# Transposing DMAs queued by ScalarE instead of SyncE, with a third column turned by DMA

## The chip, the cores and the metric

The kernel runs on one core of one Trainium2 chip. The metric is the device time of one execution in microseconds (us); the median of three executions of the kernel before is 1655.98 us (1655.0 to 1656.74).

## The reference

One layer of cross attention and one layer of an expert-choice feed-forward network, both with a residual, in float32:

```python
x = x + xattn(layernorm(x), ctx)            # x: 2 x 2048 x 512, ctx: 2 x 77 x 384, 8 heads of 64
x = x + ffn(layernorm(x))

def ffn(x, gate_w, w1, w2):                 # 8 experts, 512 -> 2048 -> 512
    probs = softmax(einsum('ntd,ed->nte', x, gate_w), -1)
    g, m = top_k(probs.transpose(0, 2, 1), k)          # k = 2 * 2048 / 8 = 512 tokens of each batch
    xin = x[batch_idx, m]
    h = gelu(einsum('nekd,edf->nekf', xin, w1))
    h = einsum('nekf,efd->nekd', h, w2)
    return zeros.at[batch_idx, m].add(g[..., None] * h)
```

A column is one (batch, expert) pair: 512 tokens, their gates, and the expert's weights. There are 16.

## The kernel before

After the attention stage the layer-normed rows lie in HBM as `xn2_rows`. The expert stage has two parts. Four columns are **plain** (`PLAIN`, experts 0 and 1 of both batches), done one after another, i = 0 to 3, each in 16 slots (n = 16 i + f, f = 0 to 15). The other six experts are done as **pairs** x = 0 to 5, both batches at once, in groups of a quarter of the hidden size (n = 0 to 23, four for each pair). All products use a high and a low part of both operands, three matmuls for one.

In a slot TensorE makes `up(n)` (12 matmuls into bank 4 or 5) and then `down(n - 2)` (12 matmuls); at f = 15 the last two down products follow at once, and at f = 0 and 1 there is none. `up(n)` waits for the gelu of slot n - 2, which frees its bank. ScalarE's order in a slot is: the high parts of the weights of slot n + 2 (`act_weights`, two copies), the gelu of slot n (line 1743), and then what else is put into that slot. VectorE makes the low parts and the low part of the gelu (line 1935), which the down product waits for.

A column's rows are gathered from HBM by GpSimd (`pool_gather`, `gather_pair`) with the token on the partition, and the products want them transposed. Column 0 and column 2 (the third) are transposed on TensorE: `pe_token_chunk` (line 1732), four transposes for each of four chunks, for the third column at the end of slots 27 to 30 (`TURNS_1`, `turn`), and ScalarE and VectorE copy each chunk out of PSUM as its high and low part (`act_token_chunk`, `dve_token_chunk`).

The keys in `TURNED` are transposed by DMA instead: columns 1 and 3, pair 0 (`(0, 1)` and `(0, 0)`, one key for each batch), and the later pairs. A DMA transposes two-byte words, so this goes in steps, each in two halves a = 0, 1 (two of the four row tiles each):

- `act_split` (line 1490): ScalarE separates the 16-bit halves of the float words into `planes`, two instructions, and raises `r_split`.
- `sp_turn` (line 1497): SyncE waits for `r_split` and issues the transposing DMA of 512 KB within SBUF, which raises `r_turn[a]` when it has landed.
- `act_words` (line 1507): ScalarE waits for `r_turn[a]` and joins the halves back into float words, four instructions; `r_word` tells that the rows are ready.
- For a plain column, `act_turned_chunk` and `dve_turned_chunk` then make the high and low parts of its four chunks.

For column i + 1 the splits stand in slots f = 10 and 11 of column i, the words in 12 and 13, the chunks in 14 and 15. For pair 0 the splits are in slots 49, 50 (batch 1) and 52, 53 (batch 0), the words in 51, 52 and 54, 55. Of a later pair, one batch each is turned in the second and third group of the pair before: after the first three weight copies of the next group comes the first split, then four more copies, the second split, and both words.

SyncE's queue is in order (`sp_experts`): weight loads (`sp_weights`, two of 1 MB for every four slots) and the transposing DMAs stand in one list. For pair 0 the transposes of a batch stand ahead of the weight loads of the fourth column's third and fourth quarter; in the late stage the loads of group n + 2 wait for the words of the key whose buffers they overwrite.

GpSimd's queue is in order as well: gathers, the scatter-adds of finished columns (line 1597), and ten lists of tokens and gates for the later pairs, each written by 16 indirect DMAs (`write_lists`, line 1612): one list, the second column's gather, two lists, scatter, one list, the third column's gather, two lists, scatter, the fourth's gather, the gather of (0, 1), three lists, the gather of (0, 0), scatter, one list.

Of the kernel before, what the change touches and what calls it, by code (L numbers as in the profile page):

```python
# [14 lines left out]
P = 128  # L15
B, S, D = 2, 2048, 512
# [25 lines left out]
def xattn_expert_choice(nc, x, ctx, wq, wk, wv, wo, bo, gate_w, w1, w2, out):  # L42
# [8 lines left out]
    with top:  # L51
# [1410 lines left out]

        r_split, r_word = sem("r_split"), sem("r_word")
        r_turn = [sem(f"r_turn{a}") for a in range(2)]
        TURNED = ((1,), (3,), (0, 1), (0, 0)) + tuple((x, b) for x in range(1, NS) for b in range(B))

        def turned(key):

# [22 lines left out]
                                            rows[:, h, 2 * a:2 * a + 2], ACT.Copy)  # L1491
            last.then_inc(r_split, 1)

        def sp_turn(sp, key, a):
            halves, out = planes_of(key)
            sp.wait_ge(r_split, turned(key) - 1 + a)
            sp.dma_start(out[:, a * 4 * CAP:(a + 1) * 4 * CAP].rearrange("p (j t) -> p j t", t=P),
                         halves[:, 2 * a:2 * a + 2].rearrange("p q c -> p (q c)"), transpose=True).then_inc(r_turn[a], 16)

        def act_words(act, key, a):  # L1500
            words = rows_of(key).bitcast(U16).rearrange("p c (q t h) -> p h q c t", h=2, t=P)
# [6 lines left out]
            last.then_inc(r_word, 1)  # L1508


        SPLIT_AT, WORDS_AT, CHUNKS_AT = (10, 11), (12, 13), {14: (0, 1), 15: (2, 3)}

        PAIR_SPLIT_AT = {(0, 1): (49, 50), (0, 0): (52, 53)}
        PAIR_WORDS_AT = {(0, 1): (51, 52), (0, 0): (54, 55)}
# [24 lines left out]

        assert rounds_in(ROUNDS_AT[-1])[1] == ROUNDS - 1  # L1540
        VALS_AT = CHOICE_AT + 4
        TURNS_1 = tuple(range(KF // 2 + 3, KF - 1))
# [4 lines left out]
        hot_of = {q: m for m, q in HOT_AT.items()}  # L1547
        found_of = {q: m for m, q in FOUND_AT.items()}

        def turn(n):  # L1550

            i, f = divmod(n, KF)
            return TURNS_1.index(f) if i == 1 and f in TURNS_1 else None

        def sp_experts(sp):
            for gg in range(2, G * len(PLAIN)):
                if gg >= 4 * G - 2:
                    for a in range(2):
                        sp_turn(sp, (0, 4 * G - 1 - gg), a)
                sp_weights(sp, gg)  # L1560
                if gg in (G, 3 * G):
                    for a in range(2):
                        sp_turn(sp, (gg // G,) if gg == G else (3,), a)
            for n in range(NG):
                e, g = NPE + n // G, n % G
                key = ((n - 2) // G + 1, (n - 2) % G - 1) if n >= 2 else None
                if key in TURNED:
                    sp.wait_ge(s_Wl, NPR * (n - 2) + 3)
                    sp.wait_ge(s_sum, 4 * (n - 1))
                    for a in range(2):  # L1570
                        sp_turn(sp, key, a)
                    sp.wait_ge(r_word, turned(key))
                if n < 2:
                    sp.wait_ge(f_w2l, NPL - GF * (1 - n))
                else:
                    sp.wait_ge(s_Wl, NPR * (n - 2) + 3)
                    sp.wait_ge(s_sum, 4 * (n - 1))
                sp.dma_start(w1_raw[:, n % 2], group_w1(e, g)).then_inc(s_raw1[n % 2], 16)
                if n >= 2:
                    sp.wait_ge(s_v2l, GF * (n - 1))  # L1580
                if key in TURNED:
                    for a in range(2):
                        sp.wait_ge(r_turn[a], 8 * turned(key))
                sp.dma_start(w2_raw[:, n % 2], group_w2(e, g)).then_inc(s_raw2[n % 2], 16)
            sp.wait_ge(s_scat, 16 * ND * NS)

        def pool_experts(pool):
# [72 lines left out]
            pool_gather(pool, 1)  # L1660
            write_lists(1, 3)
            scatter(0)
            write_lists(3, 4)
            pool_gather(pool, 2)
            write_lists(4, 6)
            scatter(1)
            pool_gather(pool, 3)
            gather_pair(0, 1)
            write_lists(6, 9)
            gather_pair(0, 0)  # L1670
            scatter(2)
            write_lists(9, 10)
            for x in range(E - NPE - LX):
                read_lists(x)
            scatter(len(PLAIN) - 1)
# [29 lines left out]
                                    ALU.subtract).then_inc(f_w2l, 1)  # L1705

        def act_token_chunk(act, i, k, bank):
            act.wait_ge(f_tr, i // 2 * KD + k + 1)
# [27 lines left out]
        def act_experts(act):  # L1736
            def slot(n):
# [10 lines left out]
                if n == 2:  # L1748
                    act_gate_exp(act, NBLK - 1)
                    act_normalise(act, X1[:, u], rs2, nb2, XN2[:, u], g_nb2, a_xn2, NBLK - 1)  # L1750
                k = turn(n - 1)
                if k is not None:
                    act_token_chunk(act, (n - 1) // KF + 1, k, 6)
                i, f = divmod(n, KF)
                if (i + 1,) in TURNED:
                    if f == SPLIT_AT[0]:
                        act.wait_ge(f_rows, 16 * CT * (i + 2))
                    if f in SPLIT_AT:
                        act_split((i + 1,), SPLIT_AT.index(f))
                    if f in WORDS_AT:  # L1760
                        act_words(act, (i + 1,), WORDS_AT.index(f))
                    for k in CHUNKS_AT.get(f, ()):
# [105 lines left out]
            def group(n):  # L1868
# [21 lines left out]
                if n + 1 < NG:  # L1890
                    for idx in W_ORDER[0:3]:
                        w_high(n + 1, idx)
                    if key in TURNED:
                        act.wait_ge(s_rows[key[1]], 16 * CT * (x + 2))
                        act.wait_ge(s_v2l, GF * (n + 1))
                        act_split(key, 0)
                    for idx in W_ORDER[3:]:
                        w_high(n + 1, idx)
                    if key in TURNED:
                        act_split(key, 1)  # L1900
                        act_words(act, key, 0)
                        act_words(act, key, 1)
                if last:
# [20 lines left out]
        def dve_experts(dve):  # L1924
            def slot(n):
# [5 lines left out]
                if n >= S3:  # L1931
# [5 lines left out]
                k = turn(n - 1)  # L1937
                if k is not None:
                    dve_token_chunk(dve, (n - 1) // KF + 1, k, 6)
                i, f = divmod(n, KF)  # L1940
                if (i + 1,) in TURNED:
                    for k in CHUNKS_AT.get(f, ()):
# [225 lines left out]
        def pe_experts(pe):  # L2168
# [33 lines left out]
            def slot(n):  # L2202
# [154 lines left out]
```

## Time and profile before

| | |
|---|---|
| median of three executions | 1655.98 us |
| the profiled execution, its own time | 1658.91 us |
| its span, first to last instruction | 1657.1 us |
| TensorE busy | 1641.7 us (99%) |
| VectorE busy | 1074.7 us (65%) |
| ScalarE busy | 942.8 us (57%) |
| GpSimd busy | 476.6 us (29%) |
| mean granted TensorE clock | 0.997 |

Busy times are of one execution. Issuing a DMA, waiting and branching are not counted as busy, though an engine that issues is held by it. Overlapping matmuls are counted once. The expert stage starts at about 305 us, the groups of pairs at about 660.

### The profile page before, as it was taken

To read this page: it belongs to the slowest core of one execution; us is meant where nothing else is said; L and a number is where in the kernel's file an instruction comes from. 1 tells how busy PE (TensorE), PEld (TensorE's weight loads), DVE (VectorE), ACT (ScalarE), POOL (GpSimd) and SP (SyncE) were. 2 spreads that over 40 slices of the span, in tenths; PEclk is the share of its full clock that TensorE was granted. 3 is DMA by queue.
4 is the path that set the end of the run, shared out by engine and by line. 5 is a ranking of instruction groups with operands and counts; after the bars stand their busy time and mean duration, and the time that the engine had idled before them with its cause. 6 is when DMAs were issued, how large, how long until landed. Compare 5 with 4: busy or idle time off the path is not lost.

```text
span 1657.1 us, 22979 instructions
## 1 busy us (share of the span) xinstructions
PE 1641.7 (99%) x8348; PEld 1405.0 (85%) x8348; DVE 1074.7 (65%) x1938; ACT 942.8 (57%) x2045; POOL 476.6 (29%) x537
## 2 busy tenths in 40 slices
PE   9999999999999999999999999999999999999997
PEld 9999999878888878888888888888888888888886
DVE  7555697777764438655765586558655856686663
ACT  5678776735333565466546664666466646654441
POOL 3233233377477770300230033003200420040003
PEclk9999999999999999999999999999999999999999
DMA  3243436365426694412442244234323432351004
GB/s 134 77 140 115 153 119 226 127 152 127 131 54 180 128 178 151 102 29 85 136 108 53 84 119 102 76 85 101 95 77 96 96 89 77 102 97 57 26 1 51
DMA packets 140357, 171.27 MB, mean 103 GB/s; under 512 B 68141, under 2 KB 69321, under 8 KB 140249
## 3 DMA queue, kind: packets, MB, share of 16 engines
q1 hardware_dynamic: 120441, 136.04, 27.5%
q0 software_dynamic: 19776, 33.78, 11.3%
q8 instruction: 65, 1.06, 0.3%
q14 instruction: 43, 0.35, 0.1%
q10 hardware_dynamic: 32, 0.03, 0.0%
HBM read 121.42 MB, written 33.72 MB: 94 GB/s over the span
## 4 chain that ended last, share of the span: by engine, by line
PE 95%; ACT 1%; DMA 1%; DVE 1%; issue 0%; POOL 0%; POOLq 0%; SPq 0%; ACTq 0%; DVEq 0%
PE ps L2282 10%; PE ps L2280 10%; PE ps L2281 10%; PE ps L2260 9%; PE ps L2258 9%; PE ps L2259 9%; PE ps L1254 4%; PE ps L1255 4%; PE ps L1256 4%; PE ps L2195 3%; PE ps L2182 3%; PE ps L2184 3%; PE ps L2183 3%; PE ps L2196 3%; PE ps L2197 3%; DMA turned_planes<-planes 1%
## 5 line engine op out<-in xcount | busy, mean ns | idle before, releaser
L2280 PE MATMUL ps<-v2h,hhS 128*128 128x512 f32 x768 | 298.9, 389 | 0.0
L2282 PE MATMUL ps<-v2h,hlS 128*128 128x512 f32 x768 | 298.9, 389 | 0.0
L2281 PE MATMUL ps<-v2l,hhS 128*128 128x512 f32 x768 | 298.9, 389 | 0.0
L1646 POOL DMA_INDIRECT out_dram<-YS,tok_pair x40 | 86.4, 2161 | 682.8 <-DVE YS L2091 673.7
L2259 PE MATMUL ps<-Tl,Wh 128*128 128x512 f32 x672 | 261.5, 389 | 0.0
L2258 PE MATMUL ps<-Th,Wh 128*128 128x512 f32 x672 | 261.5, 389 | 0.0
L2260 PE MATMUL ps<-Th,Wl 128*128 128x512 f32 x672 | 261.5, 389 | 0.0
L1612 POOL DMA_INDIRECT list<-pairs,list_at x160 | 171.1, 1069 | 49.3 <-issue 48.2
L1833 ACT ACTIVATE v2h<-w_raw 128x512 fp32r<-128x512 f32 x96 | 57.5, 622 | 215.0 <-PE ps L2282 215.0
L2281 PEld LDWEIGHTS ps<-v2l,hhS 128*128 128x128 f32 x768 | 144.2, 188 | 30.0
L2282 PEld LDWEIGHTS ps<-v2h,hlS 128*128 128x128 f32 x768 | 144.2, 188 | 29.8
L2280 PEld LDWEIGHTS ps<-v2h,hhS 128*128 128x128 f32 x768 | 144.2, 188 | 29.8
L1851 ACT ACTIVATE hhS<-hfS 128x512 fp32r<-128x512 f32 x144 | 91.0, 632 | 127.8 <-DVE hfS L2060 66.4
L2071 DVE TENSOR_TENSOR hlS<-hfS,hhS 128x512 fp32r<-128x512 f32 x192 | 128.0, 687 | 46.8 <-ACT hfS L1852 46.8
L2091 DVE SCALAR_TENSOR_TENSOR YS<-ps,tok_pair,YS 128x512 f32<-128x512 f32 x120 | 88.8, 749 | 102.2 <-PE ps L2282 102.2
L2259 PEld LDWEIGHTS ps<-Tl,Wh 128*128 128x128 f32 x672 | 126.2, 188 | 26.2
L2260 PEld LDWEIGHTS ps<-Th,Wl 128*128 128x128 f32 x672 | 126.2, 188 | 26.1
L2258 PEld LDWEIGHTS ps<-Th,Wh 128*128 128x128 f32 x672 | 126.2, 188 | 26.1
L2182 PE MATMUL ps<-eTh,w1h 128*128 128x512 f32 x248 | 98.1, 395 | 2.2 <-ACT hf L1743 2.2
L2195 PE MATMUL ps<-w2h,hh 128*128 128x512 f32 x248 | 98.1, 396 | 0.0
L1743 ACT ACTIVATE hf<-ps 128x512 f32<-128x512 f32 x64 | 38.2, 597 | 103.6 <-PE ps L2184 103.6
L2183 PE MATMUL ps<-eTl,w1h 128*128 128x512 f32 x248 | 97.1, 392 | 0.0
(297 smaller groups left out, 3692.9 us busy)
## 6 DMA issues: line engine op xcount, KB each, us to landing
w_raw<-in_L_ffn_w_dram SPq DMA_DIRECT2D x80, 1024.0 KB, 7.3
XB<-in_x_dram SPq DMA_DIRECT2D x16, 512.0 KB, 4.0
XR<-in_x_dram SPq DMA_DIRECT2D x16, 512.0 KB, 6.4
out_dram<-X SPq DMA_DIRECT2D x16, 512.0 KB, 5.0
xn_rows<-XN SPq DMA_DIRECT2D x16, 512.0 KB, 5.3
list<-pairs,list_at POOLq DMA_INDIRECT x160
w_raw<-in_L_xattn_Wq_dram SPq DMA_DIRECT2D x1, 1024.0 KB, 8.4
wo_sb<-in_L_xattn_Wo_dram SPq DMA_DIRECT2D x2, 512.0 KB, 11.0
```

The costliest lines, as they stand in the source:

```text
L1612: pool.indirect_dma_start(out=lists[b * E + NPE + LX + x], out_offset=bass.IndirectOffsetOnAxis(ap=list_at[:, b, x, t:t + 1], axis=0), in_ ...
L1851: nc.scalar.activation(hhS[:, b, f], src, ACT.Gelu)
L2071: nc.vector.tensor_tensor(hlS[:, b, f], hfS[:, b, f], hhS[:, b, f].bitcast(F32), ALU.subtract).then_inc(s_hid, 1)
L2182: nc.tensor.matmul(ps[:, 4 + n % 2, :], wh, th, start=(k == 0), stop=False)
L2183: nc.tensor.matmul(ps[:, 4 + n % 2, :], wh, tl, start=False, stop=False)
L2195: nc.tensor.matmul(ps[:, c, :], th, wh, start=(f == 0), stop=False)
L2258: nc.tensor.matmul(ps[:, bank, :], wh, th, start=(idx in OPENS and k == 0), stop=False, **go_on)
L2259: nc.tensor.matmul(ps[:, bank, :], wh, tl, start=False, stop=False, **go_on)
L2260: last = nc.tensor.matmul(ps[:, bank, :], wl, th, start=False, stop=(k == 1), **go_on)
L2280: nc.tensor.matmul(ps[:, bank, :], th, wh, start=(t == 0), stop=False)
L2281: nc.tensor.matmul(ps[:, bank, :], th, wl, start=False, stop=False)
L2282: last = nc.tensor.matmul(ps[:, bank, :], tl, wh, start=False, stop=(t == GF - 1))
```

## The change

ScalarE takes over the transposing DMAs: `sp_turn` becomes `act_turn`, and every call of `act_split` has it right behind. SyncE's list keeps the weight loads alone. The third column (key `(2,)`) joins `TURNED`: its chunks no longer pass TensorE, its splits both stand in slot 29 (f = 13 of column 1), its words in 30 and 31, its four chunks in 31. GpSimd writes two lists in place of one ahead of the third column's gather, and the last list moves from behind the third scatter to ahead of the gather of (0, 0). In the late stage ScalarE takes over SyncE's two waits for the weight buffers, for work of the group before.

```diff
-        TURNED = ((1,), (3,), (0, 1), (0, 0)) + tuple((x, b) for x in range(1, NS) for b in range(B))
+        TURNED = ((1,), (2,), (3,), (0, 1), (0, 0)) + tuple((x, b) for x in range(1, NS) for b in range(B))
...
-        def sp_turn(sp, key, a):
+        def act_turn(act, key, a):
             halves, out = planes_of(key)
-            sp.wait_ge(r_split, turned(key) - 1 + a)
-            sp.dma_start(out[:, a * 4 * CAP:(a + 1) * 4 * CAP].rearrange("p (j t) -> p j t", t=P),
+            act.wait_ge(r_split, turned(key) - 1 + a)
+            act.dma_start(out[:, a * 4 * CAP:(a + 1) * 4 * CAP].rearrange("p (j t) -> p j t", t=P),
...
-        SPLIT_AT, WORDS_AT, CHUNKS_AT = (10, 11), (12, 13), {14: (0, 1), 15: (2, 3)}
+        SPLIT_AT = {i: {13: (0, 1)} if i == 1 else {10: (0,), 11: (1,)} for i in range(3)}
+        WORDS_AT = {i: {14: (0,), 15: (1,)} if i == 1 else {12: (0,), 13: (1,)} for i in range(3)}
+        CHUNKS_AT = {i: {15: (0, 1, 2, 3)} if i == 1 else {14: (0, 1), 15: (2, 3)} for i in range(3)}
...
             for gg in range(2, G * len(PLAIN)):
-                if gg >= 4 * G - 2:
-                    for a in range(2):
-                        sp_turn(sp, (0, 4 * G - 1 - gg), a)
                 sp_weights(sp, gg)
-                if gg in (G, 3 * G):
-                    for a in range(2):
-                        sp_turn(sp, (gg // G,) if gg == G else (3,), a)
...
                 if key in TURNED:
-                    sp.wait_ge(s_Wl, NPR * (n - 2) + 3)
-                    sp.wait_ge(s_sum, 4 * (n - 1))
-                    for a in range(2):
-                        sp_turn(sp, key, a)
                     sp.wait_ge(r_word, turned(key))
...
             scatter(0)
-            write_lists(3, 4)
+            write_lists(3, 5)
             pool_gather(pool, 2)
-            write_lists(4, 6)
+            write_lists(5, 7)
             scatter(1)
             pool_gather(pool, 3)
             gather_pair(0, 1)
-            write_lists(6, 9)
+            write_lists(7, 10)
             gather_pair(0, 0)
             scatter(2)
-            write_lists(9, 10)
...
-                k = turn(n - 1)
-                if k is not None:
-                    act_token_chunk(act, (n - 1) // KF + 1, k, 6)
                 i, f = divmod(n, KF)
                 if (i + 1,) in TURNED:
-                    if f == SPLIT_AT[0]:
+                    for a in SPLIT_AT[i].get(f, ()):
                         act.wait_ge(f_rows, 16 * CT * (i + 2))
-                    if f in SPLIT_AT:
-                        act_split((i + 1,), SPLIT_AT.index(f))
...
+                        act_split((i + 1,), a)
+                        act_turn(act, (i + 1,), a)
...
                     if n in PAIR_SPLIT_AT[key]:
                         act_split(key, PAIR_SPLIT_AT[key].index(n))
+                        act_turn(act, key, PAIR_SPLIT_AT[key].index(n))
...
                         act.wait_ge(s_v2l, GF * (n + 1))
+                        act.wait_ge(s_Wl, NPR * n + 3)
+                        act.wait_ge(s_sum, 4 * (n + 1))
                         act_split(key, 0)
+                        act_turn(act, key, 0)
                     for idx in W_ORDER[3:]:
                         w_high(n + 1, idx)
                     if key in TURNED:
                         act_split(key, 1)
+                        act_turn(act, key, 1)
...
-                if turn(n) is not None:
-                    pe_token_chunk(pe, n // KF + 1, turn(n), 6)
```

## Rows read from the trace of the kernel before

**Rows 1.** The page, busy time, share and instructions of TensorE and the others.

```profile
PE 1641.7 (99%) x8348; PEld 1405.0 (85%) x8348; DVE 1074.7 (65%) x1938; ACT 942.8 (57%) x2045; POOL 476.6 (29%) x537
```

**Rows 2.** Timeline of TensorE, 603 to 615: start, us, instruction, [idle before].

```profile
603.58 0.39 PE L2182 MATMUL ps<-eTh,w1h 128*128 128x512 f32 x1
...
608.79 0.39 PE L2197 MATMUL ps<-w2h,hl 128*128 128x512 f32 x1
611.36 0.77 PE L2182 MATMUL ps<-eTh,w1h 128*128 128x512 f32 x1 [2.18 <-ACT hf L1743]
...
614.81 0.40 PE L2184 MATMUL ps<-eTh,w1l 128*128 128x512 f32 x1
```

**Rows 3.** Windows: length, PE, PEld, DVE, ACT, POOL busy, clock, DMA share, GB/s.

```profile
610.00:615.00 5.00, 3.64 (x9) 2.96 (x10) 2.32 (x4) 3.11 (x5) 0.30 (x1) 0.66 1.26 136
```

**Rows 4.** The chain of waits, 580 to 616: start, us, what.

```profile
584.51 0.52 ACT w1h L1692
...
585.55 0.49 ACT hf L1743
...
589.76 15.34 DMA turned_planes<-planes
```

**Rows 5.** Timeline of ScalarE, slots 49 to 53, for (0, 1).

```profile
582.51 2.00 ACT L1490 ACTIVATE planes<-XR 128x1024 uint16<-128x1024 uint16 x2
...
598.69 2.67 ACT L1507 ACTIVATE XR<-turned_planes 128x512 uint16<-128x512 uint16 x4 [7.91 <-DMA turned_planes<-planes]
...
610.63 0.59 ACT L1743 ACTIVATE hf<-ps 128x512 f32<-128x512 f32 x1
```

**Rows 6.** Timeline of TensorE at one of the third column's four chunks.

```profile
471.49 0.65 PE L1732 MATMUL ps<-ident,XB 128*128 128x128 f32 x4
...
472.22 0.39 PE L2183 MATMUL ps<-eTl,w1h 128*128 128x512 f32 x1
```

**Rows 7.** Transposing DMAs: issue ns min/median/max; fourth column's issue and words; SyncE's wait.

```profile
L1497 SPq DMA_TRANSPOSE w_raw<-w_raw x20: 1752/1904/2028, 732.5 to 1430.0; - x20
L1497 SPq DMA_TRANSPOSE turned_planes<-planes x8: 1987/3090/8527, 363.9 to 613.1; - x8
...
543.73 5.00 SPq L1497 DMA_TRANSPOSE turned_planes<-planes  x1
...
553.04 2.66 ACT L1507 ACTIVATE XB<-turned_planes 128x512 uint16<-128x512 uint16 x4 [0.35 <-DMA turned_planes<-planes]
...
SPq L1496 <- ACT w_raw L1490: 416.3, 10, 54.7
```

**Rows 8.** Timelines, slot 29: ScalarE's gelu, VectorE's low part; TensorE, next expert's start.

```profile
468.97 0.60 ACT L1743 ACTIVATE hf<-ps 128x512 f32<-128x512 f32 x1 [2.57 <-PE ps L2184]
...
470.14 0.69 DVE L1935 TENSOR_TENSOR hl<-hf,hh 128x512 fp32r<-128x512 f32 x1
...
489.34 0.39 PE L2182 MATMUL ps<-eTh,w1h 128*128 128x512 f32 x1
```

**Rows 9.** Timeline of ScalarE in a late group, second split to the next group.

```profile
734.37 2.00 ACT L1490 ACTIVATE w_raw<-XB 128x1024 uint16<-128x1024 uint16 x2
738.48 5.17 ACT L1507 ACTIVATE XB<-w_raw 128x512 uint16<-128x512 uint16 x8 [2.11 <-DMA w_raw<-w_raw]
749.26 1.15 ACT L1833 ACTIVATE v2h<-w_raw 128x512 fp32r<-128x512 f32 x2 [5.62 <-PE ps L2282]
```

**Rows 10.** GpSimd: third column's gather, third column's scatter, and all list writes grouped.

```profile
441.75 1.19 POOL L943 DMA_INDIRECT XB<-xn_rows,tok_idx  x1 [16.68 <-DVE tok_gate L823]
...
582.20 1.63 POOL L1597 DMA_INDIRECT out_dram<-Y,tok_idx  x1 [0.30 <-issue]
...
L1612 POOL DMA_INDIRECT list<-pairs,list_at x160 | 171.1, 1069 | 49.3 <-issue 48.2
```

**Rows 11.** Timeline at the start: first plain DMA issue on SyncE and on ScalarE.

```profile
0.81 0.42 SPq L236 DMA_DIRECT2D ctx_sb<-in_ctx_dram  x1
0.81 0.61 ACTq L417 DMA_DIRECT2D gw_sb<-in_L_ffn_gate_w_dram  x1
```

More of the change, by code:

```diff
@@ L1492, in act_split @@
             last.then_inc(r_split, 1)
-        def sp_turn(sp, key, a):
+        def act_turn(act, key, a):
             halves, out = planes_of(key)
-            sp.wait_ge(r_split, turned(key) - 1 + a)
-            sp.dma_start(out[:, a * 4 * CAP:(a + 1) * 4 * CAP].rearrange("p (j t) -> p j t", t=P),
-                         halves[:, 2 * a:2 * a + 2].rearrange("p q c -> p (q c)"), transpose=True).then_inc(r_turn[a], 16)
+            act.wait_ge(r_split, turned(key) - 1 + a)
+            act.dma_start(out[:, a * 4 * CAP:(a + 1) * 4 * CAP].rearrange("p (j t) -> p j t", t=P),
+                          halves[:, 2 * a:2 * a + 2].rearrange("p q c -> p (q c)"), transpose=True).then_inc(r_turn[a], 16)
         def act_words(act, key, a):
@@ L1541, in xattn_expert_choice @@
         VALS_AT = CHOICE_AT + 4
-        TURNS_1 = tuple(range(KF // 2 + 3, KF - 1))
         HOTS = [q for q in range(VALS_AT + 1, 3 * KF + 4)
@@ L1548, in xattn_expert_choice @@
         found_of = {q: m for m, q in FOUND_AT.items()}
-        def turn(n):
-            i, f = divmod(n, KF)
-            return TURNS_1.index(f) if i == 1 and f in TURNS_1 else None
         def sp_experts(sp):
             for gg in range(2, G * len(PLAIN)):
-                if gg >= 4 * G - 2:
-                    for a in range(2):
-                        sp_turn(sp, (0, 4 * G - 1 - gg), a)
                 sp_weights(sp, gg)
-                if gg in (G, 3 * G):
-                    for a in range(2):
-                        sp_turn(sp, (gg // G,) if gg == G else (3,), a)
             for n in range(NG):
@@ L1707, in act_token_chunk @@
         def act_token_chunk(act, i, k, bank):
-            act.wait_ge(f_tr, i // 2 * KD + k + 1)
+            act.wait_ge(f_tr, i * KD + k + 1)
             nc.scalar.activation(eTh[i % 2][:, k, :], ps[:, bank, :], ACT.Copy).then_inc(f_eTh, 1)
@@ L1750, in slot @@
                     act_normalise(act, X1[:, u], rs2, nb2, XN2[:, u], g_nb2, a_xn2, NBLK - 1)
-                k = turn(n - 1)
-                if k is not None:
-                    act_token_chunk(act, (n - 1) // KF + 1, k, 6)
                 i, f = divmod(n, KF)
                 if (i + 1,) in TURNED:
-                    if f == SPLIT_AT[0]:
+                    for a in SPLIT_AT[i].get(f, ()):
                         act.wait_ge(f_rows, 16 * CT * (i + 2))
-                    if f in SPLIT_AT:
-                        act_split((i + 1,), SPLIT_AT.index(f))
-                    if f in WORDS_AT:
-                        act_words(act, (i + 1,), WORDS_AT.index(f))
-                    for k in CHUNKS_AT.get(f, ()):
+                        act_split((i + 1,), a)
+                        act_turn(act, (i + 1,), a)
+                    for a in WORDS_AT[i].get(f, ()):
+                        act_words(act, (i + 1,), a)
+                    for k in CHUNKS_AT[i].get(f, ()):
                         act_turned_chunk(act, i + 1, k)
@@ L1936, in slot @@
                                         ALU.subtract).then_inc(f_h, 1)
-                k = turn(n - 1)
-                if k is not None:
-                    dve_token_chunk(dve, (n - 1) // KF + 1, k, 6)
                 i, f = divmod(n, KF)
                 if (i + 1,) in TURNED:
-                    for k in CHUNKS_AT.get(f, ()):
+                    for k in CHUNKS_AT[i].get(f, ()):
                         dve_turned_chunk(dve, i + 1, k)
```

## Prediction

> **What bounds the kernel now.** I read the page first: TensorE is busy for 1641.7 of 1657.1 us [rows 1], so the change can pay only by taking work off TensorE or by removing a place where TensorE waits. The waits of TensorE, next, name one such place that the change touches: the fourth expert, in the slots 51 to 55. TensorE's rows there [rows 2] show the last down product starting at 608.79 and the next up product at 611.36, where 609.02 was due (the slot from 603.58 to 608.79 has 24 matmuls, so they start 0.227 apart). That is 2.34 us idle. Then eight matmuls take until 614.81, 3.45 us where 1.82 was due, 1.63 more: the granted clock of this stretch is 0.66, between the levels of 1.2 and 2.4 GHz, and what came before it is the idle time [rows 2, 3]. Together 3.97 us. The chain of waits gives the cause [rows 4]: the second transposing DMA of pair (0, 1) took 15.34 us from issue to landing, ScalarE stood waiting for both, 7.91 us for the first alone, and so the gelu of slot 53, which frees the PSUM bank for that up product, came only at 610.63 [rows 5].
>
> The reader is to see in [rows 5] that a gelu is not needed at once. It started 0.73 us before the up product that it let go. So the gelu of slot 53 may start until 609.02 - 0.73 = 608.3 at no cost, and each slot before it until 5.44 us (24 x 0.227) earlier. All costs below are weighed against such limits.
>
> **Part 1, the third column leaves TensorE.** Four times four transposes go. One group starts at 471.49 and the second matmul after it at 472.22 [rows 6]: 0.73, where two matmuls without it are 0.23 apart, so 0.50. The three others of this kind in the trace are a little shorter; I take 0.45 each, 1.8 us in all, and this is on the path, since nothing hides TensorE's own work. **-1.8 us.**
>
> **Part 2, ScalarE queues the DMAs.** There are 28 now and 30 after. An issue held SyncE 1.75 to 2.03 us in the late stage (20 of them) and 1.99 to 8.53 us, median 3.09, in the early stage (8 of them) [rows 7]. ScalarE is now held instead. No issue on ScalarE of this kind is in the trace; of plain ones the first took 0.61 there and 0.42 on SyncE [rows 11]. So an issue in the late stage costs between 1.9 and 1.9 x 0.61 / 0.42 = 2.8 us; I take 1.9, as the same descriptors are made. The move alone lands nothing earlier: SyncE stood waiting for ScalarE's split before the first DMA of each of the ten late pairs [rows 7], not the other way round.
>
> What is held behind it on ScalarE, in the late stage: four weight copies, then the second half's split, then the words. Now the second split starts at 734.37, is done after 1.9 at 736.3, the words start at 738.48 after a wait of 2.11 for the landing, end at 743.65, and ScalarE's next work is let go by TensorE only at 749.26 [rows 9]. With two issues of 1.9 the words start at 736.3 + 3.8 = 740.1, past the landing of the first half. The first half was issued when its split was done, four copies of 0.52 before 734.37, at 732.3, so it took 6.2 to land; at that pace the second, issued at 738.2, lands at 744.4 and its words end at 746.9. Of 5.6 us of cover, 3.3 are used. With 2.8 each it still fits; from about 3.7 each on TensorE would stall in each of the ten groups. **0 us**, at both ends.
>
> By the Trainium skill (DMA: Bandwidth & Descriptors, Issuing engines are not separate DMA queues) DMAs of ScalarE and SyncE run on the same DMA engines and interleave, and issuing from both saves only issue time on a sequencer. By that rule the change has no transfer to gain here, only issue time to move onto a busier engine; SyncE's wait in [rows 7] agrees; by the rule alone the sum would be part 1, 1654.2.
>
> **Part 3, the third column on ScalarE.** Both splits and both issues now stand in slot 29, words in 30 and 31, four chunk copies in 31. With TensorE 0.9 earlier by then, slot 29's gelu is at 468.97 - 0.9 = 468.1 [rows 8]. From there gelu 0.49, split 2.0, issue j0, split 2.0, issue j1, weights 1.04, gelu, words 2.5, weights, gelu of slot 31 at 477.7 + j0 + j1 (durations from [rows 4, 5]). The next expert was at 489.34 [rows 8], now 487.5; the last down product before it starts 2.7 earlier, at 484.8, and wants the gelu 1.9 before (gelu at 468.97, VectorE's low half done at 470.83 [rows 8]), at 482.9. So j0 + j1 may be 5.2. Clean: 3.8, no cost. As in the fourth column, whose first issue took 5.00 [rows 7] and whose second, queued on an idle ring, I put at 2.5: 7.5, a stall of 2.3 and perhaps 1.6 of slow clock behind it, 3.9. SyncE's weight load of that slot is in flight then, but on its own queue; in the fourth column it stood ahead of that 5.00. I take 2.6 + 2.0 = 4.6: **0 us**, ends 0 and +3.9.
>
> **Part 4, lists.** One list more is written ahead of the third gather. GpSimd stood 16.68 us before that gather, waiting for its indices [rows 10]; a list takes 22 (171.1 and 49.3 over ten lists), so the gather and all behind it come 5 us later. Its rows are first read in slot 29, some 20 us after: nothing. But pair (0, 0)'s gather and the scatter of the third column, first issue at 582.20 [rows 10], also come 5 us later, to about 587, while the pair's splits come 1.8 earlier. The list that ran beside the pair's second transpose is gone. SyncE no longer holds the weight load behind the transposes, so it starts at about 580, beside the first one.
>
> **Part 5, the pair in slots 49 to 54.** In the old clock: split at 582.51, first issue i0 at 584.5, weights, gelu, second split, second issue i1 at 588.0 + i0, weights and gelu (1.53 per slot, [rows 4]), words of 2.5 at 593.6 + i0 + i1, then pair (0, 0)'s split and issue i2, weights, and the gelu of slot 53 at 599.2 + i0 + i1 + i2. Limit 608.3, so the three may take 9.1. Also the second transpose must land by 608.3 - 1.0 - i2 - 2.0 - 2.5 = 602.8 - i2. Bounds: all clean, 5.7, no stall. As on SyncE now, 5.2, 8.5 and 3.0, sum 16.7: 7.6 late, 9.0 by slot 54, where a fourth issue of 3.1 is added. I take the first, now ahead of the scatter, at 3.0, the second, inside it, at 5.2, the third at 1.9: 10.1, 1.0 over. Its landing, issued at 591.0, takes 9.3 (the fourth column's first half, 543.73 to 553.04 [rows 7]) to 15.3 [rows 4]: 600.3 to 606.3 against a limit of 600.9, so 0 to 5.4 late. Middle 3.0, plus 1.6 of slow clock: 4.6 against 4.0 now, **+0.6 us**. In short, the wait for the landing shrinks and the issues take its place: this is what is late next.
>
> **Sum.** -1.8 + 0 + 0 + 0.6 = -1.2 us. The profiled execution took 1658.91, 2.9 over the median 1655.98, perhaps with a longer stall; on it 1657.7, on the median **1654.8 us**.
>
> **Rivals.** *The pair's stall goes* (A): clean issues and landing under the limit; -1.8 - 4.0 = -5.8, 1650.2. For it: the list beside it and the queue ahead are gone. Against: the scatter stays. *ScalarE is held by the issues themselves* (B), slower: i0 + i1 + i2 as on SyncE, 16.7; from a sum of 13.3 on (9.1, the 4.0 of now less 1.6, and the 1.8) the kernel is slower; loss 9.0 + 1.6 against 4.0, net +4.8, 1660.8 (1662.4 with a second slow stretch). For it: 8.53 us on SyncE beside that very scatter [rows 7], and the weight load now runs beside the first one. Against: the first is out of the scatter, and ScalarE's ring holds no loads. *The third column stalls* (C): forecast + 3.9 = 1658.7. *An issue costs ScalarE over 3.7 us in the late stage* (D): at 5.0, 2.5 x 10 more, 1680; against it [rows 11].
>
> By the Trainium skill (DMA: Bandwidth & Descriptors, Queues, rings and completion order) each DMA engine takes turns between the queues that have work for it, packet by packet. By that rule the pair's transposes, now on a queue of their own, would share with the weight load instead of standing before it, which favours B's price for the first issue; no run here shows a load and a transpose on two queues.
>
> **Chances.** Forecast 0.47, A 0.24, B 0.15, C 0.11, D 0.03. Under 0.2% (3.3 us, about what a measurement of this kernel can tell from no change) lie the forecast and most of C. Faster 0.26 (A and a little of the forecast), slower 0.22 (B, D, some of C with a long pair), same 0.52. The range of 8 in 10 goes from A, 1650.2, to B, 1661; D and B's far end are left out.
>
> **What would show it.** Right: no transposes into PSUM in slots 27 to 30; transposing issues on ScalarE's queue near 1.9 us from 730 us on; in the ten late groups a wait of ScalarE for TensorE before the copy of v2h still over 2 us; TensorE idle between 600 and 620 by 1 to 5 us with the clock below 1 behind it. Wrong: no idle time there (A); early issues of 5 us and more on ScalarE with gelu of slot 51 already late (B); idle TensorE at 480 to 490 (C); TensorE waits in the late groups (D).

## The result, and the profile after

The changed kernel takes 1674.03 us (median of four executions, 1672.69 to 1674.66); the kernel before, run beside it, 1656.36 us (1655.0 to 1658.2). The ratio is 1.0105, interval 1.0087 to 1.0122: slower by about 1%, where 1654.8 was forecast with a range up to 1661.0. The profiled execution took 1674.66 us, its span is 1672.7 us against 1657.1, so 15.6 us are to be explained. (The medians differ by 17.7 us; the traced execution of the kernel before was 2.6 us above its median.)

First the page and two groups of TensorE's waits between 300 and 700 us (us in total, times, longest):

```profile
PE 1640.1 (98%) x8332; PEld 1401.3 (84%) x8332; DVE 1074.8 (64%) x1938; ACT 950.8 (57%) x2057; POOL 480.5 (29%) x537
...
PE ps L2167 <- ACT hf L1729: 13.0, 2, 9.8
PE ps L2180 <- DVE hl L1923: 3.4, 2, 2.5
```

TensorE is busy 1.6 us less than before [rows 1], and in these two groups it waits 16.4 us where [rows 2] showed one wait of 2.18. The timeline of TensorE shows the places:

```profile
476.43 0.39 PE L2167 MATMUL ps<-eTh,w1h 128*128 128x512 f32 x1
...
484.56 0.50 PE L2180 MATMUL ps<-w2h,hh 128*128 128x512 f32 x1 [2.53 <-DVE hl L1923]
...
488.45 0.50 PE L2180 MATMUL ps<-w2h,hh 128*128 128x512 f32 x1 [0.87 <-DVE hl L1923]
...
604.59 0.77 PE L2167 MATMUL ps<-eTh,w1h 128*128 128x512 f32 x1 [9.77 <-ACT hf L1729]
...
609.72 0.40 PE L2180 MATMUL ps<-w2h,hh 128*128 128x512 f32 x1
...
632.23 0.47 PE L2167 MATMUL ps<-eTh,w1h 128*128 128x512 f32 x1 [3.27 <-ACT hf L1729]
```

After the wait of 9.77 us, twelve matmuls take 609.72 - 604.59 = 5.13 us where 12 x 0.227 = 2.73 was due: 2.4 more. The windows (length; PE, PEld, DVE, ACT and POOL busy; granted clock; DMA share; GB/s) give a clock of 0.55 there, between the two levels of 1.2 and 2.4 GHz, and what came before it is the idle time, as in [rows 3]:

```profile
605.00:610.00 5.00, 5.00 (x14) 3.85 (x14) 1.41 (x4) 2.61 (x5) 0.00 (x0) 0.55 1.04 164
630.00:640.00 10.00, 7.78 (x27) 6.29 (x28) 5.48 (x10) 9.55 (x18) 0.00 (x0) 0.83 0.27 59
```

In the same way the 13 matmuls from 632.23 take 1.7 us more than due. ScalarE's timeline says what TensorE waited for (start, us, instruction, idle before):

```profile
470.46 5.95 ACTq L1497 DMA_TRANSPOSE turned_planes<-planes  x1
...
478.49 2.77 ACTq L1497 DMA_TRANSPOSE turned_planes<-planes  x1
...
586.50 16.21 ACTq L1497 DMA_TRANSPOSE turned_planes<-planes  x1
602.82 0.63 ACT L1678 ACTIVATE w1h<-w_raw 128x512 fp32r<-128x512 f32 x1 [16.34 <-issue]
...
603.87 0.58 ACT L1729 ACTIVATE hf<-ps 128x512 f32<-128x512 f32 x1
...
606.37 2.31 ACTq L1497 DMA_TRANSPOSE turned_planes<-planes  x1
...
610.26 2.67 ACT L1507 ACTIVATE XR<-turned_planes 128x512 uint16<-128x512 uint16 x4
...
618.84 1.59 ACTq L1497 DMA_TRANSPOSE turned_planes<-planes  x1
...
624.03 6.32 ACTq L1497 DMA_TRANSPOSE turned_planes<-planes  x1
```

The first issue of pair (0, 1) held ScalarE 16.21 us. Slot 50's gelu stood behind it, came at 603.87, and TensorE went on 0.72 us later. The words at 610.26 show no wait: at the pair nothing is late by landing any more, everything by issuing. The three long issues (5.95, 16.21, 6.32) are those beside which another queue had just begun. SyncE's timeline, then GpSimd's:

```profile
466.61 0.37 SPq L851 DMA_DIRECT2D w_raw<-in_L_ffn_w_dram  x1
...
584.28 0.37 SPq L851 DMA_DIRECT2D w_raw<-in_L_ffn_w_dram  x1
...
622.46 0.37 SPq L851 DMA_DIRECT2D w_raw<-in_L_ffn_w_dram  x1
...
585.47 1.15 POOL L1622 DMA_INDIRECT XB<-xn_rows,tok_idx  x1 [0.30 <-issue]
...
590.69 1.63 POOL L1584 DMA_INDIRECT out_dram<-Y,tok_idx  x1 [0.30 <-issue]
```

A load of 2 MB starts 1.6 to 3.9 us ahead of each of the three, and around the one of 16.21 us GpSimd's gather and scatter start as well. In the late groups all is quiet: twenty issues, no wait of TensorE, and ScalarE's wait for TensorE before its copy of v2h still 195.8 us in all, where it had been 215.0 in the kernel before.

```profile
L1497 ACTq DMA_TRANSPOSE w_raw<-w_raw x20: 1580/1865/2889, 747.9 to 1447.3; - x20
...
ACT v2h L1817 <- PE ps L2265: 195.8, 23, 16.7
```

The sum of the stretches: -1.9 (the third column; the up product of slot 31 starts at 476.43 where it started at 478.33, and in slot 22, at 425.35, the two timelines had been 0.06 apart), -4.0 (the wait and slow clock of before), +4.0 (third column: 3.4 idle, the rest its slower start), +9.77 + 2.4 (slot 50's gelu), +3.27 + 1.7 (slot 53's): 15.2 of the 15.6 us.

That the timelines are level in slot 22 hides one loss more. The traced execution of the changed kernel enters the expert stage 1.7 us earlier than that of the kernel before, and it gives this back behind the second column's first issue, which held ScalarE 3.57 us: VectorE, next, idled 3.29 us for ScalarE's late weight copy, and so TensorE waited for VectorE at a small matmul of the token choice.

```profile
362.19 3.57 ACTq L1497 DMA_TRANSPOSE turned_planes<-planes  x1
...
375.10 0.19 PE L694 MATMUL ps<-cnt,ones_bf 128*128 128x24 bf16 x1 [1.41 <-DVE cnt L688]
```

### The profile page after: what moved, and what is told of

Its sections match the earlier page's. It is cut to its first block, busy times and chain, and to the rows that moved or that the text cites. A ratio compares the mean times of both kernels' runs of the same rounds, so it can differ in the third digit from the quotient of the medians.

```text
span 1672.7 us, 22962 instructions
## 1 busy us (share of the span) xinstructions
PE 1640.1 (98%) x8332; PEld 1401.3 (84%) x8332; DVE 1074.8 (64%) x1938; ACT 950.8 (57%) x2057; POOL 480.5 (29%) x537
## 4 chain that ended last, share of the span: by engine, by line
PE 92%; ACT 3%; ACTq 2%; DVE 1%; issue 0%; DMA 0%; POOL 0%; POOLq 0%; SPq 0%
PE ps L2263 10%; PE ps L2264 10%; PE ps L2265 10%; PE ps L2242 9%; PE ps L2241 9%; PE ps L2243 9%; PE ps L1254 4%; PE ps L1255 4%; PE ps L1256 4%; PE ps L2167 3%; PE ps L2169 3%; PE ps L2168 3%; PE ps L2180 3%; PE ps L2182 3%; PE ps L2181 3%; ACTq L1497 2%
## 5 line engine op out<-in xcount | busy, mean ns | idle before, releaser
L1599 POOL DMA_INDIRECT list<-pairs,list_at x160 | 175.1, 1095 | 49.3 <-issue 48.2
L1817 ACT ACTIVATE v2h<-w_raw 128x512 fp32r<-128x512 f32 x96 | 57.4, 622 | 195.8 <-PE ps L2265 195.8
L2169 PE MATMUL ps<-eTh,w1l 128*128 128x512 f32 x248 | 98.0, 395 | 0.0
```

What stands on the lines that cost most here:

```text
L1599: pool.indirect_dma_start(out=lists[b * E + NPE + LX + x], out_offset=bass.IndirectOffsetOnAxis(ap=list_at[:, b, x, t:t + 1], axis=0), in_ ...
L2169: last = nc.tensor.matmul(ps[:, 4 + n % 2, :], wl, th, start=False, stop=(k == KD - 1))
```

## The experiments

The theory after this reading: what costs is that the issuing instruction lasts longer while the DMA engines are busy with other queues, and that moving it gave up an order. On SyncE's list the pair's transposes stood ahead of a weight load, which therefore began behind them; on ScalarE's they begin beside it, and ScalarE's gelu waits behind the issue. Rivals: the new list order on GpSimd; the issue on ScalarE as such; the late groups.

Beside these versions the kernel before took 1658.65 to 1659.38 us, some 3 us more than beside the changed kernel, while the expected times were set against its 1656; so each time is to be read by its ratio.

**The engine alone.** The kernel before, with `sp_turn` made `act_turn`, with the two late waits that go with it, and nothing else (third column on TensorE, lists as before).

```diff
-        def sp_turn(sp, key, a):
+        def act_turn(act, key, a):
...
                     if n in PAIR_SPLIT_AT[key]:
                         act_split(key, PAIR_SPLIT_AT[key].index(n))
+                        act_turn(act, key, PAIR_SPLIT_AT[key].index(n))
...
```

> The kernel before with one part of the change alone: ScalarE queues the transposing DMAs right behind the splits, SyncE keeps the weight loads. Third column on TensorE and lists in the old order. Theory (queueing by ScalarE beside load, gather and scatter is the loss): the pair's issues take 8 to 16 us in all more than clean ones, 1660 to 1668 us. Rival (lists in the new order bring gather and scatter onto the transposes): 1655 to 1658 us.

1670.54 us, ratio 1.0068 (1.0051 to 1.0085): the upper end of what was expected (1668 to 1656 is 1.007). The first issue of (0, 1) took 10.83 us and that of (0, 0)'s second half 5.93, each with a load begun just before (583.64 and 617.42), and TensorE waited 4.38 and 3.87 us behind them:

```profile
585.86 10.83 ACTq L1497 DMA_TRANSPOSE turned_planes<-planes  x1
...
618.99 5.93 ACTq L1497 DMA_TRANSPOSE turned_planes<-planes  x1
```

So the move of the queue alone makes the kernel slower, without lists or third column.

**The engine undone.** The changed kernel with every transpose back on SyncE; the third column's, like the pair's, ahead of the weight load of its slot.

```diff
             for gg in range(2, G * len(PLAIN)):
+                ahead = {2 * G + 1: (2,), 4 * G - 2: (0, 1), 4 * G - 1: (0, 0)}.get(gg)
+                if ahead:
+                    for a in range(2):
+                        sp_turn(sp, ahead, a)
                 sp_weights(sp, gg)
...
```

> The changed kernel with one part undone: SyncE queues all transposing DMAs again, those of the third column and of pair 0 ahead of the weight load of that slot. The third column stays off TensorE and the lists stay in the new order. Theory (ScalarE held by issues is the loss): the transposes on TensorE are saved, 1.8 us, the stall of the pair is at most the 4 us of before, so 1650 to 1655 us. Rival (the new order of lists and scatter, or the third column itself, is the loss): 1665 us or more.

1654.43 us, ratio 0.9971 (0.996 to 0.9983): faster than the kernel before, by 0.3%, and by the ratios 1.3% below the changed one. Its span is 1651.6, and TensorE's only wait in the plain columns is one of 0.2 us that the kernel before has too. SyncE's two issues of (0, 1) take 5.18 us in all with the pause between them: the load begins behind them, at 587.86, and the gather only with the second, at 586.25. Those of (0, 0) take 9.22, beside the lists that GpSimd reads; that is no shorter than in the changed kernel (1.59 and 6.32), but nobody stands behind them except the load:

```profile
582.63 5.18 SPq L1497 DMA_TRANSPOSE turned_planes<-planes  x2
601.06 9.22 SPq L1497 DMA_TRANSPOSE turned_planes<-planes  x2
```

**The late half kept, the plain columns undone.** As the last one, but the twenty late issues stay on ScalarE.

```diff
                         act_split(key, 0)
+                        act_turn(act, key, 0)
                     for idx in W_ORDER[3:]:
                         w_high(n + 1, idx)
                     if key in TURNED:
                         act_split(key, 1)
+                        act_turn(act, key, 1)
```

> The plain experts' transposes queued by SyncE, those of the third column and the pair ahead of the weight load of their slot; the late groups' twenty queued by ScalarE as in the changed kernel; the new list order and the third column by DMA kept. Theory (the late half of the change is free, because nothing else moves while those issues run, 1.6 to 2.0 us each, and ScalarE had idle time there): the same as with SyncE everywhere, 1652 to 1656, ratio to the kernel before 0.996 to 0.999, with the late issues at 1.6 to 2.1 us and no TensorE wait in the late groups. Rival (the late issues take ScalarE's time from the scaling work and cost some of the 20 x 1.8 us): 1657 to 1670.

1654.39 us, ratio 0.9974 (0.9964 to 0.9984), the same as with SyncE throughout. Twenty of the thirty issues may stand on either engine. The whole loss is in the ten of the plain columns.

**A transfer put beside the late issues.** The changed kernel, with two copies of 1 MB in HBM that nobody reads, begun by SyncE as each late pair's first half is split.

```diff
...
                 if key in TURNED:
+                    sp.wait_ge(r_split, turned(key) - 1)
+                    for h in range(2):
+                        sp.dma_start(spare[h], w2_flat[h]).then_inc(s_spare[h], 16)
                     sp.wait_ge(r_word, turned(key))
```

> The changed kernel with a cost added to measure it by itself: in the ten late groups with transposes SyncE also queues two copies of 1 MB within HBM when the first split is done, so that their packets run beside the transposing DMAs that ScalarE queues; nothing else of the late stage uses the DMA engines then but the weight loads behind the words. Theory (turns between queues, packet by packet): the late issues of 1.6 to 2.0 us grow to 3 to 7 where the copy runs beside them, and the landing comes later by as much. Rival (only GpSimd's gather and scatter hold an issue): they stay at 1.6 to 2.0 us.

The first issue of each late pair now takes 5.58 to 5.80 us, one 10.50; the median over all twenty (first halves and second) goes from 1865 to 5042 ns:

```profile
L1497 ACTq DMA_TRANSPOSE w_raw<-w_raw x20: 1770/5042/10497, 746.6 to 1456.2; - x20
```

So the length of an issue is made by what else is under way, in a place where it had been about 1.9 us. TensorE waited 1.91 us behind the issue of 10.50, for which VectorE had stood 7.26 us without ScalarE's weight copy; 0.46 and 0.83 us came some 30 us behind two other pairs of issues, and their cause was not followed. So the cover of a late group holds one issue of 5.6 us. The time, 1679.87 us, is one execution; its ratio to the kernel before is 1.0123 where the changed kernel has 1.0105, some 3 us more, and the three waits add up to 3.2.

**Loads held until the landing.** The changed kernel, with SyncE's load of the three slots waiting for both transposed halves; then, in addition, GpSimd's scatter waiting for those of (0, 1); then, apart from these, GpSimd's gather and scatter held and the loads free.

```diff
+                behind = {2 * G + 1: (2,), 4 * G - 2: (0, 1), 4 * G - 1: (0, 0)}.get(gg)
+                if behind:
+                    for a in range(2):
+                        sp.wait_ge(r_turn[a], 8 * turned(behind))
                 sp_weights(sp, gg)
```

> The changed kernel, ScalarE queues, but SyncE issues three of its weight loads (those of slots 29, 49 and 53) only after both halves of the transposes of that stretch have landed. Theory (the DMA engines take turns between the queues packet by packet, so each 256-byte packet of a transpose waits behind a 2-KB packet of the load, and ScalarE is held until about 700 of the 2048 are through): the third column's first issue falls from 5.95 to 1.6 to 2.5 us, pair (0, 0)'s second from 6.32 to under 2.5, pair (0, 1)'s first from 16.2 to 5 to 9, since gather and scatter remain; 1653 to 1661 us. Rival (GpSimd's gather and scatter alone hold it): pair (0, 1)'s first issue stays over 12 us, and 1664 us or more.

1666.6 us, ratio 1.0049 (1.0029 to 1.0069), by the ratios 0.56% less than the changed kernel; 1661 or less was expected. The issues became short: (2,)'s first 1.94 instead of 5.95, (0, 1)'s first 1.94 instead of 16.21. The second is below the 5 to 9 expected, as GpSimd's gather began only behind it, at 587.86. But (0, 1)'s second half, begun into the gather and scatter, took 6.62 to issue, and its words waited for the landing:

```profile
584.93 1.94 ACTq L1497 DMA_TRANSPOSE turned_planes<-planes  x1
...
590.53 6.62 ACTq L1497 DMA_TRANSPOSE turned_planes<-planes  x1
...
607.50 2.65 ACT L1507 ACTIVATE XR<-turned_planes 128x512 uint16<-128x512 uint16 x4 [4.62 <-DMA turned_planes<-planes]
```

TensorE waited 7.99 us at 618.13. Next, the scatter held too:

```diff
             gather_pair(0, 0)
+            for a in range(2):
+                pool.wait_ge(r_turn[a], 8 * turned((0, 1)))
             scatter(2)
```

> As the kernel with the loads held, and GpSimd issues the third column's scatter, too, only after both halves of pair (0, 1) have landed; the gather of (0, 0) stays beside them. Theory: all early issues under 4 us, idle TensorE in slots 51 to 55 under 2 us, 1649 to 1654 us. If the first issue of the pair still takes over 8 us, neither loads nor scatter are its cause.

1660.52 us, ratio 1.0018 (1.0002 to 1.0034), a further 6 us less, but 1654 was missed: the load and the scatter that had been held began together at 602.4 and 603.1, and (0, 0)'s first issue, 606.96, fell between them with 7.69 us; TensorE waited 9.47 us at 616.47 (in the traced execution, whose 1665.01 us are 4.5 above the median, so how much of this wait the median one has is not shown). The other way round:

```diff
             write_lists(7, 10)
+            for a in range(2):
+                pool.wait_ge(r_turn[a], 8 * turned((0, 1)))
             gather_pair(0, 0)
```

> The changed kernel, but GpSimd's gather of (0,0), and what is behind it, wait until both transposed halves of (0,1) have landed; SyncE's load of that slot is not held, so the first issue of (0,1) has one other queue beside it where it had two. Theory (the issue is held until about a third of its packets have gone, and the packets take turns with each queue that has some): the first issue of (0,1), 16.2 us with two queues beside it, 5.0 to 8.5 us, as the two that had the load alone beside them (5.95 and 6.32); TensorE's wait of 9.8 us behind it under 2.5 us; the time 1659 to 1667, as what remains is the third column's and (0,0)'s long issues. Rival (the weight load alone holds it): over 12 us, and the time over 1670.

(0, 1)'s first issue took 7.44 us, as expected with one other queue beside it where there were two, and TensorE waited 0.99 us behind it. The time was not as expected: 1673.18 us, ratio 1.009 (1.0072 to 1.0108). The held gather came late for (0, 0)'s split (a wait of 2.46 us), and (0, 0)'s issues took 4.52 and 6.78:

```profile
589.08 7.44 ACTq L1497 DMA_TRANSPOSE turned_planes<-planes  x1
...
614.72 4.52 ACTq L1497 DMA_TRANSPOSE turned_planes<-planes  x1
...
622.84 6.78 ACTq L1497 DMA_TRANSPOSE turned_planes<-planes  x1
...
621.07 0.77 PE L2169 MATMUL ps<-eTh,w1h 128*128 128x512 f32 x1 [6.05 <-ACT hf L1731]
```

In these three, each issue of the third column and the pair is short where nothing is begun beside it and long where something is; holding a transfer moved the meeting to the next transpose.

**The order given back to ScalarE.** SyncE's three loads wait until ScalarE has begun the slot behind the second issue: behind the issues, not behind the landing, as on SyncE's own list.

```diff
+                behind = {2 * G + 1: 29, 4 * G - 2: 50, 4 * G - 1: 53}.get(gg)
+                if behind:
+                    sp.wait_ge(f_w1h, behind + 4)
                 sp_weights(sp, gg)
```

> The changed kernel, ScalarE queueing every transpose, but SyncE's weight load of the third column's slot and of the pair's two slots waits until ScalarE has begun the slot after the second half's issue, so that the load stands behind both issues, as it does on SyncE's own queue in the kernel before, but not behind their landing. Theory (what was lost is the order that one queue gave, not the engine): (2,)'s two issues 1.9 to 2.5 us each, the first of (0,1) 1.9 to 3, its second 2 to 5 (beside the scatter), those of (0,0) 2 to 6; TensorE's waits from 430 to 700 us 0 to 3 in all where the changed kernel has 16; the time 1652 to 1658. Rival (ScalarE pays for any queueing, since its scaling work stands behind each issue): waits over 5 us in spite of short issues, and 1660 to 1668.

1668.26 us, ratio 1.0063 (1.0047 to 1.008); both theories are missed in part. The third column is clean (1.86 and 2.07 us, no wait of TensorE). (0, 1)'s second issue fell into GpSimd's gather and scatter, took 5.59 us and landed 18.6 us after its start; TensorE's one wait there, 9.0 us, comes mainly from that landing, not from ScalarE's own work as the rival had it:

```profile
581.90 1.85 ACTq L1497 DMA_TRANSPOSE turned_planes<-planes  x1
...
587.41 5.59 ACTq L1497 DMA_TRANSPOSE turned_planes<-planes  x1
...
606.05 2.63 ACT L1507 ACTIVATE XR<-turned_planes 128x512 uint16<-128x512 uint16 x4 [7.34 <-DMA turned_planes<-planes]
```

So the gather was put behind the second issue too:

```diff
             write_lists(7, 10)
+            pool.wait_ge(f_w1h, 54)
             gather_pair(0, 0)
```

> As the version whose three weight loads stand behind both issues of their slot, and in addition GpSimd's gather of (0,0), with the scatter behind it, begins only when ScalarE has begun the slot after (0,1)'s second issue. So ScalarE queues every transpose, and nothing of another queue is begun between a pair's first issue and the end of its second. Theory (order alone was lost; ScalarE as the queueing engine costs nothing once the order is back): both issues of (0,1) 1.7 to 2.5 us, landed within 10 us, TensorE's wait of 9.0 us at 615.56 gone or under 2, the time 1651 to 1657, as the version with SyncE queueing (ratio 0.997). Rival (a stall stays wherever the pair is queued by ScalarE, since the second half is queued a ScalarE slot later): a TensorE wait over 4 us between 585 and 640, and 1659 to 1668.

1658.12 us, ratio 0.9996 (0.9987 to 1.0006): the loss is gone, with ScalarE still queueing all thirty. (0, 1)'s issues take 1.86 and 1.81 us. What keeps it 0.25% behind the version on SyncE is, by this trace, (0, 0)'s first issue, beside the scatter and the lists' reading, 4.13 us, TensorE's wait of 3.12 us behind it and a slow stretch (granted clock 0.66 from 610 to 615):

```profile
581.05 1.86 ACTq L1497 DMA_TRANSPOSE turned_planes<-planes  x1
586.57 1.81 ACTq L1497 DMA_TRANSPOSE turned_planes<-planes  x1
602.86 4.13 ACTq L1497 DMA_TRANSPOSE turned_planes<-planes  x1
...
608.81 0.47 PE L2171 MATMUL ps<-eTh,w1h 128*128 128x512 f32 x1 [3.12 <-ACT hf L1733]
```

The theory holds for (0, 1) and the third column, but the ratio of 0.997 that it expected is missed; the rival's wait of over 4 us does not come, though one of 3 us stays.

**The two companions apart, on SyncE.** The kernel before with the new list order alone, and the version with SyncE with the old list order.

```diff
-            write_lists(3, 4)
+            write_lists(3, 5)
             pool_gather(pool, 2)
-            write_lists(4, 6)
+            write_lists(5, 7)
...
-            write_lists(6, 9)
+            write_lists(7, 10)
             gather_pair(0, 0)
             scatter(2)
-            write_lists(9, 10)
```

> The kernel before with nothing but the new order of the list writes and of scatter 2. Theory: TensorE's stall at 608.79 and 611.36 in the kernel before came from the transposed halves of the pair landing late beside gather and scatter; the new order puts the gather some 5 us later, past the first half's issue, so the pair's first half lands earlier and most of those 4.0 us go: 1651 to 1656. Rival (the order does nothing for the time, and the gain of the version with SyncE comes from the third column alone): 1656 to 1659, with the same TensorE waits between 603 and 615 as before.

1661.09 us, ratio 1.0019 (1.0006 to 1.0033): not faster, as the theory had it, and not the kernel before with its old waits either, as the rival had it. The third column's rows now came late for TensorE's own transposes, which stand earlier than the DMA path's splits. The traced execution took 1665.75 us, 4.7 over the median, so how much of these waits the median one has is not shown:

```profile
PE ps L1731 <- DMA XB<-xn_rows,tok_idx: 4.0, 1, 4.0
PE ps L2181 <- ACT hf L1742: 2.8, 2, 2.6
```

Then the version with SyncE and the old list order:

> The version with SyncE queueing everything, but with the list order of the kernel before: so only the third column's rows by a DMA transpose ahead of its weight load, and the pair's ahead of theirs as before. Theory: 1.8 us less than before from TensorE's sixteen transposes, and the stall around 608 to 611 as before (some 4 us): 1654 to 1657.5. Rival (the third column carries the whole gain of the version with SyncE): 1650 to 1653.5, without TensorE waits between 603 and 615.

1660.61 us, ratio 1.0007 (0.9993 to 1.0021): no change, the rival's whole gain is excluded. From slot 22 to slot 31 TensorE gains 1.85 us, and the pair, with gather and scatter still beside it, loses that again in two waits of TensorE, 6.0 us in all:

```profile
PE ps L2173 <- ACT hf L1741: 6.0, 2, 3.0
```

Neither companion pays alone; together, with SyncE queueing, they bring the 0.3%. The traces suggest why: the column by DMA lets its rows come later, and with the later lists the gather begins at 586.25, beside the last of (0, 1)'s issues (582.63 to 587.81), where without them gather and scatter run from 576.53 to 590.28 and the issues, 581.42 to 592.83, fall into them.

## Why the prediction was wrong, point by point

**Part 1** was right: -1.8 forecast, 1.84 measured between slots 22 and 31.

**Part 2** was right: the late issues took 1.58 to 2.89 us, median 1.865, and cost nothing (the run with the late half alone). Its limit, 3.7 us for each of two issues, was too low: with the copies a group with issues of 5.77 and 4.50 us cost no wait, and one with 10.50 cost 1.91.

**Part 4** was right on what comes later, though the third column's gather came 8.7 us later (450.47 against 441.75) and not 5, which cost nothing, and on the load's early start "beside the first one"; part 5 then gave that start no price.

**Part 5** is where it failed: the first issue i0 was put at 3.0 us, "now ahead of the scatter", with 5.2 as its upper end, and took 16.21. The 5.2 came from SyncE, where the load stood behind the transpose. The move of the queue took this order away, and the bound was read from rows in which it still held. The gather of (0, 0), which stands right ahead of that scatter, had no price either; it now began at 585.47, beside the issue. Apart they cost less: with the load alone beside it the issue took 7.44 us and TensorE waited 0.99, and with the load held and the gather not yet begun it took 1.94. The method of limits was right. Slot 50's gelu might start until 608.3 - 3 x 5.44 = 592.0, and it stands 584.5 + i0 + 1.04, so i0 had 6.5 us; 16.21 is 9.7 more, and TensorE idled 9.77. The second and third issue, put at 5.2 and 1.9, took 2.31 and 1.59: the traffic had passed while the first stood. The 3.0 for the landing did not come, as the words found both halves landed. The fourth, for which 3.1 stood only in a remark, met the next load, 6.32, and cost 3.27 + 1.7.

**Part 3** failed at the same point: "in flight then, but on its own queue" was taken as a reason for 2.6 us; the issue took 5.95. The limit was right again: 5.95 + 2.77 = 8.7 against 5.2, 3.5 over, 3.4 idle.

**No part** priced the issues of the second and fourth column, which moved to ScalarE as well. The fourth's, 1.65 and 1.97 us, cost nothing; behind the second's first TensorE waited 1.41 us.

**The rivals.** B had the mechanism, ScalarE held by its own issues, and C the third column's stall; both came, so they add: at the pair B's 9.0 + 1.6 - 4.0 = 6.6 against a measured 17.1 - 4.0 = 13.1, at the third column C's 3.9 against 4.0. B was mis-sized by its first issue for the same reason as the forecast. They were weighed as alternatives, though one cause, a load that is no longer behind the transposes, is in both.

By the Trainium skill (DMA: Bandwidth & Descriptors, Queues, rings and completion order) queues with work take turns at an engine packet by packet; the prediction weighed this for B and gave it no price of its own. If the profile's packets are the page's, the trace of after agrees for the five microseconds shown below, 294, 301 and 319 packets. Beside the load alone no turns are seen at first: 713 packets of the load passed and none of the transpose; whether the transpose had any ready by then is not shown.

## What to carry to other kernels

Before a DMA is moved to another engine's queue, list what stood behind it in the old one: an in-order queue is also a schedule, and what it held back will start beside the DMA. An issue of a large transposing DMA is to be priced by what is under way when it begins, not by its kind, and it belongs on an engine that has nothing urgent behind it, or behind a wait that gives the order back; the limit until which each following instruction may start tells how long it may take. Two edits that seem to be separate, a cheaper path and a later arrival, may pay only together.

## What the runs showed of the hardware

The issuing instruction is no fixed cost: for the same 512 KB it lasted 1.58 to 16.21 us on ScalarE. Part of the DMA's packets pass while it lasts. Views of the DMA queues in four stretches (packets, MB, share of the 16 engines): from 595 to 600, inside the issue of 16.21 us; from 624.03 to 628, the first 4 us of the issue of 6.32 us beside a load, and from 624.03 to 630.35, the whole of it; and from 747.9 to 752.5, from an undisturbed late issue on (1.87 us).

```profile
q0 software_dynamic: 294, 0.81, 58.1%
q1 hardware_dynamic: 301, 0.61, 36.5%
q10 hardware_dynamic: 319, 0.08, 7.8%
...
q1 hardware_dynamic: 713, 1.43, 97.5%
...
q1 hardware_dynamic: 1020, 2.03, 94.0%
q10 hardware_dynamic: 291, 0.07, 5.2%
...
q10 hardware_dynamic: 2080, 0.52, 59.8%
```

The queue q10 carries the transposes in packets of about 250 bytes, q1 the load in packets of 2 KB, q0 GpSimd's. Undisturbed, all 2080 packets of a transpose pass within 4.6 us of the issue's start, the first of them after 1.1 us; beside the load and GpSimd's traffic, 319 in 5 us. Beside the load alone they start late: in the first 4 us of that issue 713 packets of the load pass and none of the transpose, and it is the same in the issue of 5.95 us, 505 and none from 470.46 to 475 (with 3 of GpSimd's). Why is not shown. What the end of an issue waits for stays open too; it is no fixed share of the packets, as 149 had gone in the issue of 5.95 us, 291 in that of 6.32, 698 in that of 16.21 and 549 in the undisturbed 1.9 us.

By the Trainium skill (DMA: Bandwidth & Descriptors, Issuing engines are not separate DMA queues) the sequencer's time to initiate a DMA is usually small beside the DMA itself. Here the measurement decides: 1.87 of some 4.6 us undisturbed, and 16.21 us where two other queues were at work.
